# A four-layer gated cross-attention kernel on one core: unread full-array products ahead of the maxima of the many-headed attentions and of a pass's first transposes

## The reference, cut to what matters

```python
x = x + tanh(g_xattn[0]) * L0_xattn(layernorm(x), ctx)   # 32 score heads of 8 features, differences of pairs
x = x + tanh(g_ffn[0])   * L0_ffn(layernorm(x))          # three cycles of a small net
x = x + tanh(g_xattn[1]) * L1_xattn(ctx, layernorm(x), mask)   # 8 heads of 64, 512 keys
x = x + tanh(g_ffn[1])   * L1_ffn(layernorm(x))          # 8 routed and 2 shared experts, all computed
x = x + tanh(g_xattn[2]) * L2_xattn(layernorm(x), ctx, ctx)    # 16 heads of 16
x = x + tanh(g_ffn[2])   * L2_ffn(layernorm(x))          # 16 heads of 8, then 8 experts
x = x + tanh(g_xattn[3]) * L3_xattn(layernorm(x), ctx, ctx)    # one head of 256
x = x + tanh(g_ffn[3])   * L3_ffn(layernorm(x))          # values rounded to an 8-bit float format
```

## Time and profile before

| | before |
|---|---|
| median of 3 runs | 5651.34 us (5632.83 to 5652.76) |
| profiled execution | 5660.27 us, of which the span of the instructions is 5658.5 us |
| mean granted clock of TensorE | 0.921 |
| PE busy, DVE busy, ACT busy | 86%, 49%, 33% of the span |

### The profile page before, as it was taken

How to read it: one execution, slowest core, us unless ns; L and a number is a source line. 1 busy time by engine, 2 the same in 40 slices (tenths; PEclk the granted TensorE clock), 3 DMA queues, 4 the chain that set the end, 5 groups by cost and what they waited for, 6 DMA issues and landing times.

```text
span 5658.5 us, 74258 instructions
## 1 busy us (share of the span) xinstructions
PE 4888.0 (86%) x29184; PEld 3477.8 (61%) x29184; DVE 2758.3 (49%) x7346; ACT 1853.5 (33%) x3068; POOL 95.5 (2%) x180
## 2 busy tenths in 40 slices
PE   2898878989799897998979988899888998889988
PEld 1556765567656685565855658556585565855657
DVE  3535455354553545436454454544545445454454
ACT  2422324233242333423233242332424324242242
POOL 0000000000000000000000000000000000000000
PEclk9898989999899898998989989799897998989989
DMA  6000210002000020000200002000020000200002
GB/s 273 1 1 22 88 50 1 1 22 112 26 1 1 22 112 26 1 9 21 105 26 1 15 23 97 26 1 14 31 90 26 1 22 23 90 26 1 22 23 94
DMA packets 47155, 218.95 MB, mean 39 GB/s; under 512 B 4544, under 2 KB 16832, under 8 KB 27072
## 3 DMA queue, kind: packets, MB, share of 16 engines
q1 hardware_dynamic: 46784, 213.90, 10.2%
HBM read 192.91 MB, written 20.97 MB: 38 GB/s over the span
## 4 chain that ended last, share of the span: by engine, by line
PE 70%; DVE 19%; ACT 5%; issue 3%; DMA 2%; SPq 0%; POOL 0%; DVEq 0%; ACTq 0%
PE w L418 16%; PE w L428 10%; DVE mx L1023 6%; PE o L559 6%; PE w L675 6%; PE w L517 5%; PE w L667 4%; PE w L408 4%; PE w L531 4%; PE o L552 4%; PE w L484 2%; ACT oth L786 2%; PE w L534 1%; PE w L571 1%; PE w L467 1%
## 5 line engine op out<-in xcount | busy, mean ns | idle before, releaser
L824 ACT ACTIVATE pt<-w 128x1024 f32<-128x1024 f32 x640 | 653.8, 1024 | 768.6 <-PE w L534 440.4
L1023 DVE TENSOR_REDUCE mx<-w 128x4 f32<-128x1024 f32 x512 | 593.7, 1218 | 171.9 <-PE w L467 155.1
L559 PE MATMUL o<-pt,va 128*32 128x256 f32 x4096 | 559.5, 410 | 18.7 <-ACT pt L824 18.7
L786 ACT ACTIVATE oth<-w,res 128x256 f32<-128x256 f32 x656 | 264.1, 475 | 731.0 <-PE w L667 599.8
L1259 DVE TENSOR_REDUCE mx<-w 128x2 f32<-128x1024 f32 x128 | 156.9, 1226 | 527.0 <-PE w L519 527.0
L418 PE MATMUL w<-xnT,res 128*128 128x256 f32 x1408 | 375.3, 418 | 33.8 <-ACT xnT L778 24.5
L667 PE MATMUL w<-qsp,ksp 128*128 128x256 f32 x2048 | 350.3, 289 | 0.0
L418 PEld LDWEIGHTS w<-xnT,res 128*128 128x128 f32 x1408 | 281.3, 208 | 98.8 <-issue 47.6
L559 PEld LDWEIGHTS o<-pt,va 128*32 128x32 f32 x4096 | 207.9, 114 | 194.1 <-issue 67.8
L467 PE MATMUL w<-ksp,qsp 32*128 32x256 f32 (+1 forms) x2048 | 260.9, 401 | 73.5 <-DVE mx L1023 41.5
L418 PE MATMUL w<-xnT,stream 128*128 128x256 f32 x1280 | 311.8, 391 | 0.0
(11 more groups left out here) (235 smaller groups left out, 7506.6 us busy)
## 6 DMA issues: line engine op xcount, KB each, us to landing
stream_lo<-split SPq DMA_DIRECT2D x64, 1024.0 KB, 4.8
ksp<-split SPq DMA_DIRECT2D x64, 1024.0 KB, 6.9
stream<-in_moe_dram SPq DMA_DIRECT2D x80, 384.0 KB, 3.6
va<-in_moe_dram SPq DMA_DIRECT2D x8, 1024.0 KB, 10.3
split<-ksp SPq DMA_DIRECT2D x8, 1024.0 KB, 5.6
split<-qsp SPq DMA_DIRECT2D x8, 1024.0 KB, 8.0
res<-in_resident_dram SPq DMA_DIRECT2D x1, 8157.5 KB, 22.1
cx<-in_ctx_dram SPq DMA_DIRECT2D x16, 256.0 KB, 3.6
```

The source lines that it names most:

```text
L559: mm = pe.matmul(o[g:g + 32, 0:T], by_heads(plan, s)[:, kt, plan.v_of(h), :], pt[:, n % EXPS, a * 512 + kt * T:a * 512 + (kt + 1) * T], st ...
L786: h = act.activation(dst[:, c, :], w[:, c * T:(c + 1) * T], func, bias=bias[:, c:c + 1], **more)
L824: act.activation(pt[:, n % EXPS, :], w[:, :], ACT.Exp, scale=scale).then_inc(S["s_P"], 1)
L1023: dve.tensor_reduce(mx[s][:, :, 2 * u:2 * u + 2].rearrange("p t a -> p a t"), w[:, :].rearrange("p (a t k) -> p a t k", a=2, t=TT), AX_X, ...
```

## The change

A new helper on TensorE issues products that nobody reads. Each has an 8-bit 128x128 stationary operand and an 8-bit moving operand of 512 columns, both views of `w2q`, and writes the first 512 columns of the buffer `w` that the step has just taken. The step's own first product there starts a new sum and overwrites them. One such product is put into each unit of `max` of `l0`, `l2` and `f2`, behind the wait of `take` and ahead of the wait for the first unit's queries and keys: (16 + 8 + 8) units x 2 slots = 64 per pass, 512 in all. Sixteen are put in front of `ctxT` of slot 0, ahead of the wait for the context's DMA: 128 in all. Nothing is removed, and no wait is added or moved.

```diff
@@ the TensorE block @@
+            def keep_busy(w, times):
+
+                for _ in range(times):
+                    pe.matmul(w[:, 0:512], w2q[:, 0, 0:P], w2q[:, 0:2, :], start=True, stop=True)
+
@@ spread_attention @@
                 elif what == "max":
 
                     w = take(st + ".max", s, u)
+                    keep_busy(w, 1)
                     if u == 0:
                         pe.wait_ge(*after("s_qsp", st + ".qs", s, 1))
                         pe.wait_ge(*after("s_ksp", st + ".ks", s, 1))
@@ the loop over the passes @@
                     if step == "ctxT":
 
                         w = take("ctxT", s)
+                        if s == 0:
+                            keep_busy(w, 16)
                         pe.wait_ge(s_cx[s], 16)
                         filled(transpose_features(w, cx[s]))
```

## The result

| | before | changed |
|---|---|---|
| median | 5643.52 us (5632.83 to 5652.76, 4 runs) | 5732.22 us (5724.88 to 5747.79, 4 runs) |
| ratio | | 1.0155, 95% interval 1.0132 to 1.0179 |
| profiled execution | 5660.27 us | 5747.79 us |

The change makes the kernel 88.7 us slower, where 51 us less were forecast. The time lies above the range given, and 6 us from the rival in which the clock stays down.

What follows compares the result with a forecast made beforehand. The kernel was taken as matmul-bound, paced by TensorE, whose mean clock was 0.921. The terms +55 + 8 - 2 - 112 = -51 us took the profiled 5660.27 to 5609, or 5600 as median; range 5530 to 5690.

Steps and rivals of the forecast that it cites:

- the rival in which the clock stays down: Rival: one product per unit does not change the clock granted to TensorE; costs remain, 5738 us; chance 0.17.
- What the clock gives back: Term: in the attentions of l0, l2 and f2, 373 of 557 us of low clock end, worth -112 us.
- lone maxima: Term: slot 0's 256 units of max, where added products mostly hide behind VectorE's reductions: +8 us.
- rate of 0.30 us per us of low clock: Step: time regained per us of low clock ended, taken between 0.25 from whole passes and 0.4 from l0's stretches.
- The sixteen: Term: products in front of slot 0's ctxT at pass starts, mostly in 3.65 us taken as free: -2 us.
- interleaved maxima: Term: slot 1's 256 units of max beside slot 0's exp and pv, product almost wholly on the path: +55 us.
- Exposed loads: Rival: weight loads around the product in interleaved units are not overlapped, +51 us; sum 0, 5651 us; chance 0.13.

Runs made afterwards that it cites:

- e2: The changed kernel without the sixteen products in front of ctxT, so only the 512 in the units of max: 5739.89 us, 1.0171 to the kernel before.
- e3: The kernel before plus one product in each of slot 0's units of max only, 256 in all: 5674.53 us, 1.0053 to the kernel before.
- e4: The kernel before plus one product in each of slot 1's units of max only, 256 in all: 5655.64 us, 1.0034 to the kernel before.
- e10: The kernel before plus 49 products per pass in idle waits and six in slot 1's first units of max in l0 and l2: 5551.05 us, 0.9843.
- e8: The kernel before plus 31 products per pass, all ahead of waits in which TensorE idled: 5589.64 us, 0.9906 to the kernel before.
- e1: The kernel before plus only the sixteen products in front of slot 0's ctxT, none in the maxima: 5650.67 us, 1.0022 to the kernel before.

## Why the prediction was wrong

**What the clock gives back** is the step that failed, -112 us for 373 us of low clock. In the passes 174 us ended. I had let the tails and the interleaved stretches end, and the lone maxima and l0's rest stay. In l0 it was the other way round: the lone maxima lost 6.8 us of low clock per pass, which is worth nothing there, and the rest all of its 5.7, while the tail kept its 10.8 and the interleaved stretch lost only 3.7 of 13.0. In l2 the tail lost 5.2 and the interleaved stretch its 6.0. f2's interleaved stretch, high before, got 4.6 us of new low clock. I treated each stretch as if it stood alone, while the low time moves along: held up in one stretch, the clock falls in the next. e2 against e3 and e4 shows it (both sets of products together end less than either alone), and e10 the reverse.

What it gave back is read from the lengths, over eight passes: 19 us in l0's rest, 5 in l2's tail, and 17 in the interleaved stretches. The last is 37.5 us of low clock at 0.44, the rate of the changed kernel's l0 stretch, which takes 32.8 us where all is high and 37.3 with 10.2 low. That is 41 us instead of 112, 71 of the 138 us between forecast and profile. l0's tail, as low as before, is 6 us longer.

The rate of 0.30 us per us of low clock was near as a mean, but it is not one number. Within e4's runs it is 0.39, in the interleaved stretch 0.44. In the tails, where TensorE waits for VectorE and ACT in between, e8 gives 2.1 us for 8.7, 0.24, and l2's tail in the changed kernel 5 us for 40. In e8's f2 maxima 3.1 us of low clock ended for nothing.

**The lone maxima** were to hide behind VectorE, +8 us. They lengthened by 1.4, 1.9 and 1.5 us per pass in the changed kernel, 38 us in eight: 30 us of the gap. At low clock a unit with its product takes 0.54 + 0.72 = 1.26 us (2958.44 and 2957.18 in the timeline are 1.26 apart), above VectorE's 1.14. The prediction had the 1.25, but took the excess as rare, while l2's units nearly all ran so (9.9 of 10.7 us low).

**The sixteen** were to cost -2 us. They cost 5.1 us per pass and gave 2.5 back behind, 17 us in seven passes. The trace of the changed kernel:

```profile
2916.79 0.52 POOL L1368 MEMSET va<- 128x512 f32 x1 [168.98 <-SPq L1453]
...
2920.32 6.55 PE L408 MATMUL w<-w2q 128*128 128x512 fp8e4 x16 [10.08 <-issue]
...
2926.70 0.60 PE L413 MATMUL w<-res,cx 128*128 128x128 f32 x4
...
2927.99 1.99 PE L423 MATMUL w<-ctxT,res 128*128 128x256 f32 x8 [0.69 <-ACT ctxT L786]
```

With nothing to wait for, TensorE's first instruction comes 3.53 us after POOL's. Before, its first transposes came 3.65 us after the earlier trace rows. Over passes 2 to 8 it is 3.53 to 3.97 us in the changed kernel and 3.25 to 3.87 in e1. So the 3.65 us that I took as free were, but for 0.3 us at most, not idle for the DMA: in e1 its data landed at most 0.31 us behind the first product. The row named the DMA because that ended last. All the products stood on the path. The clock's gift behind them, 2.2 us forecast, was 2.5. Over whole runs e1 is only 8.3 us slower, so some more comes back later in the pass.

**The interleaved maxima** were priced at 55 us. The stretches grew by 46 us over eight passes, and the clock's 17 us come on top: 63 us, about 0.25 each. At 0.32 and 0.54 us instead of 0.24 and 0.45, and with the overlap at its neighbours lost, the price should have been higher; some of it presumably falls into gaps, which no run separates. That the size was near is luck as much as working. Exposed loads were the right mechanism and worth less here than the 51 us of that rival. Of the rival in which the clock stays down the time is near, 5738, but not the working: the clock did rise, in the wrong places, and the lone maxima cost three times its 13 us.

The terms, measured in the profiles: 63 + 38 + 17 for the products, -41 for the clock and +6 for l0's tail, 83, against 87.5.

## What to carry to other kernels

Low clock costs most where TensorE is the bound and little where it waits for another engine, so look for the place where the low stretch ends up and not where it begins. Count it in the passes: a mean over the whole program can contain a setup in which it costs nothing. Put unread products first into waits in which TensorE is idle anyway, counted so that they end before the wait does, and check in a trace that the wait isn't the engine's own late start. Among products that share the array by row groups, a full-array product is a barrier that costs 0.1 us even when it is short, and the kernel's own products of both kinds show that price before anything is added. A few at the point just before the clock falls were worth more than one in every unit.

## What the runs showed of the hardware that I had not expected

One product of 64 columns on the full array between 32-row products costs 0.115 us, of which its columns are 0.03 by the estimate above and lost clock another 0.03. Two products per unit did no worse than one, and probably better, because the clock then held in all of l0's interleaved stretches. And TensorE starts 3.25 to 3.97 us later than POOL at a pass's start, with nothing to wait for; no run here tells why. Sixteen products ahead of that start do not carry the clock over it.
